# Turning and multiplying the small weights earlier inside a two-layer graph kernel's adjacency loop

## The reference

```
A = scatter_add(edge_weight at [src, dst]); deg = row sums; A_norm = dinv * A * dinv
h = x; for l in 0, 1:  h = A_norm @ h;  h = h @ W_gcn[l] + b_gcn[l]
                       h = leaky_relu(h @ W_mlp[l] + b_mlp[l])
x = layernorm(x + h)
x = layernorm(x + GCNConv(relu(GCNConv(x, W1, b1)), W2, b2))   # counts of edges, self-loops
```

## Time and profile before

| | |
|---|---|
| time of three runs | 334.63, 334.9, 335.05 us; median 334.9 |
| the profiled execution's own time | 335.47 us |
| its span, first to last instruction | 333.6 us |
| granted TensorE clock | 0.997 |
| PE / DVE / ACT busy | 314.5 / 189.0 / 122.0 us |

### The profile page before, as it was taken

The page is one execution under the profiler, slowest core; times in us unless marked ns, Lnnn a source line. Parts: engine busy times, 40 slices in busy tenths (PEclk is TensorE's granted clock), DMA queues, the critical chain, the costliest instruction groups (busy, mean ns, idle before and its releaser), DMA issues.

```text
span 333.6 us, 4919 instructions
## 1 busy us (share of the span) xinstructions
PE 314.5 (94%) x1977; PEld 259.7 (78%) x1977; DVE 189.0 (57%) x333; ACT 122.0 (37%) x253; POOL 49.9 (15%) x54
## 2 busy tenths in 40 slices
PE   2878999998999999999999999999999999999993
PEld 1767786876788888888888888888888888888882
DVE  6998999714544611165643457675953444225664
ACT  3637889546434401134432013233702444220000
POOL 2100000001005970100000011121680000001111
PEclk9999999999999999999999999999999999999998
DMA  6270000700000000000700000006100000000121
GB/s 211 66 254 2 3 2 0 249 6 2 3 0 1 2 0 0 2 0 0 238 15 0 2 0 0 0 4 226 61 2 0 0 0 2 0 4 33 63 84 73
DMA packets 8590, 13.43 MB, mean 40 GB/s; under 512 B 1906, under 2 KB 2290, under 8 KB 8564
## 3 DMA queue, kind: packets, MB, share of 16 engines
q1 hardware_dynamic: 8564, 13.05, 11.6%
HBM read 10.95 MB, written 2.10 MB: 39 GB/s over the span
## 4 chain that ended last, share of the span: by engine, by line
PE 88%; DVE 7%; issue 2%; ACT 1%; DMA 1%; POOLq 0%; POOL 0%; SPq 0%; ACTq 0%
PE psum L650 75%; PE psum L708 6%; PE psum L636 3%; DVE hot L1004 2%; PE psum L755 1%; DVE sel L996 1%; PE psum L830 1%; DVE hot L999 1%; PE psum L692 1%; DVE wm_low L1089 1%; DVE wgt_low L1076 1%; PE psum L714 1%; DMA src_i<-in_src 1%; PE psum L864 1%; ACT hot L455 0%
## 5 line engine op out<-in xcount | busy, mean ns | idle before, releaser
L441 POOL TENSOR_TENSOR small<-small 128x1 f32<-128x1 f32 x16 | 11.9, 742 | 161.6 <-DVE small L1272 161.6
L708 PE MATMUL psum<-hot,sel 128*128 128x96 bf16 x512 | 32.3, 215 | 2.1 <-DVE hot L1004 1.3
L708 PEld LDWEIGHTS psum<-hot,sel 128*128 128x128 bf16 x512 | 28.4, 101 | 7.5 <-issue 6.9
L650 PE MATMUL psum<-at_high,x_high 128*128 128x512 f32 x64 | 25.8, 403 | 0.6 <-DVE x_low L1200 0.6
L1076 DVE SCALAR_TENSOR_TENSOR y_low<-psum,small,y_high 128x512 fp32r<-128x512 f32 x16 | 11.9, 750 | 24.2 <-ACT y_high L455 24.2
L650 PE MATMUL psum<-at_low,x_high 128*128 128x512 f32 x64 | 25.1, 392 | 0.0
L650 PE MATMUL psum<-y_high,at_high 128*128 128x512 f32 x64 | 25.0, 391 | 0.0
L650 PE MATMUL psum<-cnt,x_high 128*128 128x512 f32 x64 | 25.0, 390 | 0.0
L650 PE MATMUL psum<-at_high,x_low 128*128 128x512 f32 x64 | 25.0, 390 | 0.0
L650 PE MATMUL psum<-cnt,x_low 128*128 128x512 f32 x64 | 25.0, 390 | 0.0
L650 PE MATMUL psum<-y_low,at_high 128*128 128x512 f32 x64 | 24.9, 390 | 0.0
(11 more groups left out here) (185 smaller groups left out, 755.3 us busy)
## 6 DMA issues: line engine op xcount, KB each, us to landing
wg_raw<-in_L_gnn_W_gcn SPq DMA_DIRECT2D x2, 1024.0 KB, 5.5
x_raw<-in_x SPq DMA_DIRECT2D x1, 2048.0 KB, 10.3
xs<-in_x SPq DMA_DIRECT2D x1, 2048.0 KB, 9.3
w_raw<-in_L_gnn_W SPq DMA_DIRECT2D x2, 1024.0 KB, 8.1
out<-xs SPq DMA_DIRECT2D x8, 256.0 KB, 2.0
wm_raw<-in_L_gnn_W_mlp SPq DMA_DIRECT2D x1, 1024.0 KB, 8.2
wm_next<-in_L_gnn_W_mlp SPq DMA_DIRECT2D x1, 1024.0 KB, 8.8
bias_bc<-in_L_gnn_b SPq DMA_DIRECT2D x1, 256.0 KB, 8.2
```

The costliest lines, as they stand in the source:

```text
L441: pool.tensor_tensor(r[:, 1:2], r[:, 0:1], power[:, 0:1], ALU.pow).then_inc(rstd_ready, 1)
L650: ins = pe.matmul(dest, s, m, start=first and n == 0, stop=end and n == len(pairs) - 1, skip_group_check=True)
L708: ins = pe.matmul(sums[1 if k == 0 else 0], stationary, moving, start=False, stop=False, skip_group_check=True)
```

## The change

It changes `SHARED` so that VectorE makes all five operations of batches 4 and 5. All four turns of the first layer's `W_gcn` and the first two clears go ahead of chunk 0 (a new place `FIRST`); all four parts of `wgt0` and `wm0` are lowered ahead of batch 2 (the third batch of columns). The fillers, the register loads and VectorE's order are laid out anew; the second layer's parts are lowered ahead of batch 6.

```
-    SHARED = {4: {21: 6, 27: 10}, 5: {40: 16}, 7: {66: 8, 73: 8}}
+    SHARED = {7: {66: 8, 73: 8}}
...
-        fillers = {3: [("wgt0", 0, 0, KD)], 10: [("wgt0", 1, 0, KD), ("wgt0", 2, 0, KD)], 15: [("wgt0", 3, 0, KD)],
-                   27: [("wc0", 0, 0, KD)], 31: [("wc0", 1, 0, KD), ("prep", 4, 0, KD)], 34: [("wc0", 2, 0, 2)],
-                   40: [("wc0", 2, 2, KD), ("wc0", 3, 0, 2)], 47: [("wc0", 3, 2, KD), ("bias0", 0, 0, KD)],
-                   53: [("biasb0", 0, 0, KD), ("wgt1", 0, 0, KD), ("wgt1", 1, 0, KD)],
-                   60: [("wgt1", 2, 0, KD), ("wgt1", 3, 0, KD)], 66: [("bias1", 0, 0, KD)],
-                   73: [("biasb1", 0, 0, KD), ("wc1", 0, 0, 2)], 79: [("wc1", 0, 2, KD)], 86: [("wc1", 1, 0, 2)],
-                   92: [("wc1", 1, 2, KD)], 99: [("wc1", 2, 0, 2)], 105: [("wc1", 2, 2, 3)], 112: [("wc1", 2, 3, KD)],
+        FIRST = -1
+        fillers = {FIRST: [("wgt0", i, 0, KD) for i in range(KD)],
+                   7: [("wc0", 0, 0, KD)], 8: [("wc0", 1, 0, KD)], 15: [("wc0", 2, 0, 2)], 21: [("wc0", 2, 2, KD)],
+                   27: [("wc0", 3, 0, KD)], 31: [("bias0", 0, 0, KD), ("prep", 4, 0, KD)],
+                   34: [("biasb0", 0, 0, KD), ("wgt1", 0, 0, KD), ("wgt1", 1, 0, KD)],
+                   40: [("wgt1", 2, 0, KD), ("wgt1", 3, 0, KD)], 60: [("wc1", 0, 0, KD)], 63: [("bias1", 0, 0, KD)],
+                   66: [("wc1", 1, 0, 1)], 73: [("biasb1", 0, 0, KD)], 79: [("wc1", 1, 1, 3)], 86: [("wc1", 1, 3, KD)],
+                   92: [("wc1", 2, 0, 1)], 99: [("wc1", 2, 1, 3)], 105: [("wc1", 2, 3, KD)],
                    CH - 1: [("wc1", 3, 0, KD)]}
...
-        loads = {15: [16], 31: [32], 47: [48, 64], 73: [80], 86: [96], 105: [112]}
+        loads = {15: [16], 27: [32], 31: [48], 60: [64], 63: [80], 79: [96], 99: [112]}
...
-                if c == 3:
-                    split_wm(0, range(3))
-                if c == closing[0]:
-                    split_wm(0, range(3, KD))
-                if c == 47:
+                if c == FIRST:
+                    split_wm(0, range(KD))
+                if c == 31:
                     split_wm(1, range(KD))
...
             load_offsets(0)
+            for r in range(2):
+                clear(r)
+            for name, i, k0, k1 in fillers[FIRST]:
+                filler(name, i, k0, k1)
...
-                    if opening[r] == c:
+                    if r >= 2 and opening[r] == c:
                         clear(r)
```

More of the change, by code:

```diff
@@ L1096, in _ @@
             make_all(1)
+            for i in range(KD):
+                lower_fill("wgt0", i)
+            lower_wm(0)
             make_all(2)
[L1098 to L1105, removed]
+            lower_fill("wc0", 0)
+            make_all(3)
+            lower_fill("wc0", 1)
             make_all(4)
+            lower_fill("wc0", 2)
             check_windows()
@@ L1109, in _ @@
             make_hw()
-            lower_fill("wc0", 0)
-            lower_fill("wc0", 1)
+            lower_fill("wc0", 3)
             make_all(5)
+            add_ends(0)
             take_flag()
-            lower_fill("wc0", 2)
-            add_ends(0)
+            lower_wm(1)
+            for i in range(KD):
+                lower_fill("wgt1", i)
             make_all(6)
[L1117 to L1125, removed]
             add_ends(1)
+            make_all(7)
+            lower_fill("wc1", 0)
             make_all(8)
-            make(9, 0)
-            make(9, 1)
             add_ends(2)
-            for k in range(2, 5):
-                make(9, k)
-            lower_fill("wc1", 0)
+            make_all(9)
             lower_fill("wc1", 1)
```

## The result

The changed kernel takes 345.9 us against 335.0: the ratio is 1.0325, 95% interval 1.0295 to 1.0355, so about 3.3% slower. The three executions behind it took 345.04, 345.88 and 346.56 us, a wider spread than the kernel before has (334.63 to 335.16); a fourth took 375.14 us at a mean granted clock of 0.84 and is left out (with it the median is 346.2). The forecast was 342.3 with a range up to 344.5. The direction and the largest wait were right; the time lies outside the range. The profiled execution took 346.56 us with a span of 344.8.

The account below looks back on a forecast made before the run. TensorE, busy 94% of the span, was taken to bound the kernel. Terms -3.3 + 5.4 + 0.4 + 2.35 + 1.6 = +6.45, plus 0.9 for pace, gave +7.4: 342.3 us, range 337.5 to 344.5.

Parts of the forecast that it names:

- the flag's bank: At chunk 34, wgt1 block 1 claims prep's bank 5 and waits for VectorE's flag; TensorE stands still 5.4 us.
- the clears without a filler: Clears after chunks 47, 53 and 112, no longer hidden by a filler, wait for ACT: 0.8 + 0.8 + 0.75 = 2.35 us.
- The 32 scalings taken off ACT: Scalings leaving ACT (8.8 us) were said to lie beside TensorE: nothing gained.
- the two clears now start near 6.1, when the last table copy is there: Loop start: clears end before W_gcn lands, turns start at 8.0, degrees end at 35.6.
- the lead: At the end of the degrees, the changed kernel was to be 3.3 us ahead of the kernel before.
- the slow restart: Behind the standstill at chunk 34, TensorE was to run at a slower pace at first: +0.9 us.
- bank 7: After chunk 40, block 3 wants bank 7 and waits for block 0's low part behind wm1: another 0.4 us.
- The bound of 1.5: Upper bound of the pace loss behind the 5.4 us gap, from about 3.1 us of start work taking 1.5 longer.
- The text said of the x load only that it lands in time: Load of x, late in the loop: lands 10 us behind the last scaling, so no wait.
- this batch's due time: Batch 6 ends at 52.6 for wc1 0 at 52.7, batch 9 at 75.9 for 79.3: no wait.
- ACT's queue at chunks 76 to 83: TensorE waits for ACT at the clears for 76 and 83 and scalings at 80: 1.6 us, bounds 0 and 2.2.
- the half pace also strikes at chunk 7: Rival, chance 0.10: after 2.1 us idle at chunk 7, two wc blocks run near half pace, about 2.8 on the path: 345.1.

Follow-up runs that it names:

- Experiment 1: Changed kernel with VectorE's take_flag put ahead of batch 5 and add_ends(0), nothing else; 345.35 us, ratio 1.0298 to the kernel before.
- experiment 9: Kernel before with batch 4's third product made by VectorE instead of ACT's 16 scalings at chunks 21 and 27; 334.87 us, ratio 0.9988.
- experiment 2: Changed kernel with TensorE's first register load (16 offsets) moved from ahead of the first two clears to behind the four turns; 344.28 us, ratio 1.0270.
- experiment 6: Kernel of experiment 5 with the first register load behind the four turns and the load of x held until region 14 closes; 337.76 us, ratio 1.0072.
- experiment 4: Changed kernel with 24 added zero-weight matmuls of 512 columns ahead of the turn that waits for the flag at chunk 34; 342.70 us, ratio 1.0223.
- Experiment 3: Changed kernel with the 2 MB load of x held back until region 14 is closed at chunk 99; 345.35 us, ratio 1.0305.
- experiment 5: Changed kernel with take_flag ahead of batch 5, second-layer turns 1 to 3 at chunks 47 and 53, and some low parts lowered earlier; 340.73 us, ratio 1.0159.

## Why the prediction was right and wrong

**Right: the flag's bank.** The step "wgt1 block 1 has 5, the bank of prep" gave 5.4 us, measured 5.42. Experiment 1 shows what was argued beside it: the flag is only the first door in VectorE's queue, and the wait of 5.16 moves with it. Right too were the clears without a filler (0.75, 0.65 and 0.75 against 0.8, 0.8, 0.75). The 32 scalings taken off ACT were put at nothing for TensorE; for the 16 of batch 4, experiment 9 finds 0.4 us.

**Wrong: the start.** The step that failed is "the two clears now start near 6.1, when the last table copy is there". The sum costed the clears and turns and left out the register load in front of them, although the rule of counting what an instruction is queued behind applied to it. The clears start at 8.12, the turns at 9.80 instead of 8.0, and all four take 3.4 us at the slow pace, not three. The degrees end at 37.7 instead of 35.6, so the lead was 38.9 - 37.7 = 1.2 us and not 3.3: 2.1 us of the miss. Moving the load gives 1.3 of it back in experiment 2, where W_gcn landed late, and 1.8 in experiment 6 (degrees' end at 35.86), where it did not; the last 0.3 fits the pace of the turns. In the kernel before the register load is hidden behind batch 0 on VectorE, whose end releases the first clear in the earlier trace rows, so no row showed it.

**Wrong in size: the slow restart.** The term was 0.9, with 0.4 for bank 7 beside it; measured are 2.7 in place of both: 0.42 and 0.78 on the turns, 1.21 on six chunks, 0.29 on the next two. The mechanism was right and experiment 4 shows it. The bound of 1.5 came from the start of the loop, where 3.1 us were seen slow; this time 5.9 us were, from 44.77 until the grant rose at about 50.7. It had fallen early in the wait, at about 40.5. The Trainium skill, TensorE: Matmul & The Clock Gate (The HAM clock gate), says that an idle TensorE falls to half clock and that sustained work restores it. The rows 0.50 from 42 to 50 us agree, and here, unlike at the start, the grant shows it.

**Missed: the instruction refill.** The text said of the x load only that it lands in time. In both kernels chunk 99 runs inside that load (issued at 58.31 and 70.17, landing 10.3 and 10.1 us later), but TensorE now stood 1.54 us, against 0.39 at the same chunk and 0.24 at chunk 106 in the kernel before: +0.9. The 0.24 stands right behind the register load of chunk 105 and may be that. Experiment 3 ties the gap to the load. Its size goes with how soon TensorE runs out of work behind the instruction packet: 1.0 us in the changed kernel (76.1 to 77.05), 2.1 us before (64.6 to 66.75). What sets the start of the packet was not tested.

**Missed: bank 5 once more.** The first quarter of wc1 1 at chunk 66 claims the bank of wc1 0, whose low part stands behind batch 7: 0.57. The prediction counted this batch's due time and not the part behind it.

**Too high: ACT's queue at chunks 76 to 83.** 1.6 was taken near the full bound; about 0.4 was seen, 0.13 at chunk 80 and 0.26 at the clear for chunk 83, and nothing at the clear for chunk 76. TensorE asked later than had been worked out: the 0.57 at chunk 66 lies ahead of these.

Together: 7.35 forecast + 2.1 + 1.4 + 0.9 + 0.57 - 1.2 - 0.2 (the three clears) + 0.2 (the last clear, 0.88 against 0.65) = 11.1, where 11.2 was measured. Four of these terms add in one direction, and it was luck that the fifth took 1.2 back. The range had not allowed for them: the 1.2 at its upper end fits what the pace (1.5 - 0.9) and ACT's queue (2.2 - 1.6) could still add, with nothing for the start.

**What stays open.** The executions of the changed kernel differ by 1.5 us. In single profiles the grant also fell at about 17 us, at the wait at chunk 7 (experiments 3 and 5), behind the gap at chunk 99 (experiment 1) and at the clear for chunk 76 (experiments 5 and 6), and in others with nearly the same gaps it did not. So the rival "the half pace also strikes at chunk 7" is true of some executions and not of others; what decides it was not settled.

## What to carry to other kernels

Before work is moved forward in a queue, follow through each resource it claims (here a bank taken in turn) to the engine that frees it, and to everything ahead of that in that engine's order; opening one door only shows the next. Count every instruction that stands ahead of the moved one, the register loads too: what hid them may stay behind. And a long wait on TensorE costs twice, once as idle time and again as half pace behind it: 5.9 us of work at half pace, 2.7 us lost, behind the 5.42 us here, and 3.4 us of such work behind the 5.16 of experiment 1. Several short waits can be cheaper than one long one of the same sum: those of 0.65 to 0.88 us at the clears left the changed kernel's grant at 1.00. They are not safe, though: behind one of 1.14 us in experiment 5 the grant fell.

## What the runs showed of the hardware that was not expected

- After an idle time of 5.42 us TensorE ran at the 1.2 GHz level for another 5.9 us of work; the grant had fallen 1.2 us into the wait. In experiment 1 it fell only at the end of a wait of 5.16 us, and the slow work lasted 3.4 us. 24 matmuls with zero weights in the gap kept the grant at 1.00, and with the gap at chunk 99 gone as well the kernel was 3.2 us faster.
- After gaps of 1.1 to 1.2, of 1.8 to 1.9 and of 2.2 to 2.4 us the clock fell in some executions and not in others (512-column matmuls 0.43 us apart against 0.23).
- At the same chunk TensorE's stand without a releaser was 0.39 us, 1.54, 1.84 or nothing. It was nothing when a 2 MB load was held back, and also when the instruction packet ahead of the chunk started 1.4 us before that load was issued (66.5 against 67.88 in experiment 4). In the ten traces with a stand beside that load, TensorE went on 2.3 to 2.6 us after such a packet started.
- A load of 16 registers on TensorE held the next matmul for 1.6 to 2.0 us (8.12 against 6.48 and 6.09 in experiments 2 and 6), and for 1.23 and 0.75 behind queued turns.
